# A third kind of attention step for the end: scores and one row unit together, then values, then down-projection in strips

## What is computed

```python
xn = _layernorm(x)
x = x + attn(xn) + ffn(xn)
# attn: 32 query heads and 8 key/value heads of 16; q, k, v, o are "bitnet" linears:
#   y = xn @ sign(w / s).T * (s * scale), s = max(mean(|w|), 1e-8) by row
#   scores = q k^T / 4; softmax over 1024 keys; out = softmax @ v; then the o linear
# ffn: silu(xn @ gate_w.T) * (xn @ up_w.T) @ down_w.T, inner width 1792
```

## Time and profile before

| | |
|---|---|
| median of 3 runs | 507.96 us (506.63 to 508.73) |
| the profiled execution | 507.6 us, its span 505.9 us |
| PE busy | 484.0 us, 96% of the span |
| DVE busy | 417.1 us, 82% |
| ACT busy | 352.4 us, 70% |
| POOL busy | 93.6 us, 18% |
| granted TensorE clock, mean | 0.999 |

### The profile page before, as it was taken

How to read it: one execution, slowest core, us unless ns; L and a number is a source line. 1 busy time by engine, 2 the same in 40 slices (tenths; PEclk the granted TensorE clock), 3 DMA queues, 4 the chain that set the end, 5 groups by cost and what they waited for, 6 DMA issues and landing times.

```text
span 505.9 us, 9735 instructions
## 1 busy us (share of the span) xinstructions
PE 484.0 (96%) x3882; PEld 160.9 (32%) x3882; DVE 417.1 (82%) x487; ACT 352.4 (70%) x655; POOL 93.6 (18%) x138
## 2 busy tenths in 40 slices
PE   1899999999999999999999999999999999999996
PEld 1564434434332222222222222222222223223442
DVE  7879869676779999999999999999999942223985
ACT  1943633352339999999999999999999987774000
POOL 4212244434333000000000000000000113241021
PEclk9999999999999999999999999999999999999999
DMA  8844763732005602111120220210210214452321
GB/s 275 270 86 101 164 143 43 203 67 38 6 0 75 113 26 61 41 51 36 41 61 24 43 60 23 63 40 23 62 41 24 67 36 112 110 144 78 105 72 54
DMA packets 31300, 38.99 MB, mean 77 GB/s; under 512 B 6608, under 2 KB 20816, under 8 KB 31256
## 3 DMA queue, kind: packets, MB, share of 16 engines
q1 hardware_dynamic: 22232, 27.34, 18.7%
q0 software_dynamic: 8304, 10.95, 11.6%
q10 hardware_dynamic: 720, 0.08, 0.1%
HBM read 33.24 MB, written 10.35 MB: 86 GB/s over the span
## 4 chain that ended last, share of the span: by engine, by line
PE 82%; ACT 8%; DMA 5%; DVE 2%; issue 2%; SPq 0%; ACTq 0%; DVEq 0%
PE ps L1219 24%; PE ps L1091 19%; PE ps L1184 14%; PE ps L1100 9%; PE ps L1152 8%; ACT room L674 6%; PE ps L1070 3%; PE ps L1245 3%; DMA o_scratch<-osb 2%; ACT osb L685 1%; DMA ga<-r_scratch 1%; PE ps L1008 1%; DMA hlo<-x 1%; DVE stats L733 1%; PE ps L1062 1%
## 5 line engine op out<-in xcount | busy, mean ns | idle before, releaser
L807 DVE TENSOR_REDUCE nmx<-ps 128x1 f32<-128x1024 f32 x256 | 293.7, 1217 | 14.5 <-PE ps L1100 14.3
L674 ACT ACTIVATE room<-ps 128x512 f32<-128x512 f32 x512 | 274.2, 597 | 21.2 <-PE ps L1184 11.2
L1219 PE MATMUL ps<-room,vcur 128*32 128x256 f32 (+1 forms) x1912 | 160.0, 406 | 4.4 <-ACT osb L685 4.1
L1184 PE MATMUL ps<-qst,kB 50*128 50x512 f16 x512 | 150.0, 383 | 1.0 <-DVE room L906 0.5
L1100 PE MATMUL ps<-kA,qst 48*128 48x512 f16 x512 | 145.2, 382 | 0.0
L1091 PE MATMUL ps<-room,wf 128*128 128x512 f16 x448 | 100.6, 379 | 0.0
L1219 PEld LDWEIGHTS ps<-room,vcur 128*32 128x32 f32 x1912 | 37.6, 107 | 99.7 <-issue 53.0
L1184 PEld LDWEIGHTS ps<-qst,kB 50*128 50x128 f16 x512 | 30.9, 93 | 113.0 <-ACT room L674 101.8
L655 ACT ACTIVATE room<-ps,gsc 128x512 f32<-128x512 f32 x28 | 19.2, 686 | 61.9 <-PE ps L1091 61.9
L1091 PEld LDWEIGHTS ps<-room,wf 128*128 128x128 f16 x448 | 42.4, 98 | 55.1 <-issue 7.2
L513 POOL TENSOR_TENSOR hlo<-room,hhi 128x512 f16<-128x512 f32 x28 | 34.0, 1216 | 87.7 <-ACT hhi L585 87.7
(11 more groups left out here) (127 smaller groups left out, 267.0 us busy)
## 6 DMA issues: line engine op xcount, KB each, us to landing
qst<-q_scratch SPq DMA_DIRECT2D x32, 192.0 KB, 3.6
o_scratch<-osb SPq DMA_DIRECT2D x16, 256.0 KB, 2.3
q_scratch<-parts SPq DMA_DIRECT2D x12, 256.0 KB
hlo<-x SPq DMA_DIRECT2D x8, 256.0 KB, 4.6
parts<-x POOLq DMA_DIRECT2D x8, 256.0 KB, 3.7
wf<-gate POOLq DMA_DIRECT2D x14, 128.0 KB, 4.2
wf<-up POOLq DMA_DIRECT2D x14, 128.0 KB, 5.5
wd<-down POOLq DMA_DIRECT2D x1, 1792.0 KB, 14.0
```

The source lines that it names most:

```text
L674: nc.scalar.activation(probs[:, s % 2, r, :], ps[:, score_bank(entry(j, i)), :], ACT.Exp, scale=gam_reg[par][r]).then_inc(scores_free, 1)
L807: nc.vector.tensor_reduce(nmx[:, hf, idx:idx + 1], bank_pair(idx % 2), AX.X, ALU.max, negate=True).then_inc(rows_free, 1)
L1184: nc.tensor.matmul(ps[:, score_bank(e), :], kB[low:low + SROWS, par, kt % (TT // 2) * P:(kt % (TT // 2) + 1) * P], qst[low:low + SROWS, pa ...
L1219: mm = nc.tensor.matmul(ps[32 * r:32 * r + 32, 7, of], vcur[:, par, key_tile(r, j), :], probs[:, s % 2, r, of], start=(j == 0 and part == ...
```

## The change

From step 107 on (`LATE`) a third kind of step, `late_scores`, takes the place of the others. It issues four scores (banks 4, 5, 6 and 3), then, up to step 116, one row unit (always banks 0 and 1), then all values, then as many down matmuls as `QUOTAS` says: 3 in each of steps 107 to 114, 2 in 115 and 116, 7 in 117 to 124, then 10, 9 and 9. Each of these down matmuls becomes four (`down_strips`) with 32 output columns each, which write 32 partitions of the bank each. Tiles 0 and 2 go to bank 2, tiles 1 and 3 to bank 1.

The 10 row units that steps 107 to 111 held two at a time are now in steps 107 to 116 one at a time, so the last block's maxima are transposed in step 116 (`LATE_T_STEP`) and not in 113. With that, POOL issues unit 1 ahead of the split of the last maximum, and SP stores block 13 before it waits for the last shift. VectorE takes finished down tiles at 21, 25, 29 and ahead of that step's row unit. The output projection's first four tiles use the banks in the order 0, 3, 2, 1, and wait for what used them last.

```diff
-    D_OUT = [20, 24, 28]
+    D_OUT = [21, 25, 29]
+    LATE_SCORES = [4, 5, 6, 3]
+    LATE_T = 0
+    LATE_T_STEP = 4
+    FILL_BANKS = [2, 1]
+    O_BANK = [0, 3, 2, 1]
+    LATE = (NG - 1) * STEPS - 5
+    ROWS_END = LATE + (2 * NG * UNITS - 2 * UNITS - 2 * LATE)
+    QUOTAS = [3] * 8 + [2] * 2 + [7] * 8 + [10, 9, 9]
...
@@ sync: half_ended
-                if not last or par == 0:
+                if not last or (par == 0 and hf == 0):
                     load_shift(v + 2, 1 - par, hf)
                 sp.wait_ge(pv_free, v + 3)
                 sp.dma_start(o_scratch[bass.ds(g * (REP * 2 * D), REP * 2 * D), hf * HALF:(hf + 1) * HALF],
                              osb[:, hf, :]).then_inc(osb_free[hf], 16)
+                if last and par == 0 and hf == 1:
+                    load_shift(v + 2, 1 - par, hf)
@@ gpsimd
-            normalize_io(pool, 0)
+            for u in range(2):
+                normalize_io(pool, u)
             split_max(2 * NG - 1, 1)
-            for u in range(1, QT - 1):
+            for u in range(2, QT - 1):
                 normalize_io(pool, u)
@@ vector: step_rows
+                if step < LATE:
                     row_max(ga_ * (2 * UNITS) + hf * UNITS + 2 * j, hf, 2 * j)
                     row_max(ga_ * (2 * UNITS) + hf * UNITS + 2 * j + 1, hf, 2 * j + 1)
+                elif step < ROWS_END:
+                    unit = 2 * UNITS + LATE + step
+                    dve.wait_ge(rows_ready, unit + 1)
+                    nc.vector.tensor_reduce(nmx[:, 1, unit % UNITS:unit % UNITS + 1], bank_pair(0), AX.X, ALU.max,
+                                            negate=True).then_inc(rows_free, 1)
@@ tensor
+            def down_strips(i, f, part):
+
+                if f == 0 and part == 0:
+                    if i == 0:
+                        pe.wait_ge(wd_loaded, 16)
+                        pe.wait_ge(rows_free, 2 + 2 * UNITS + 2 * LATE)
+                    elif i == 1:
+                        pe.wait_ge(rows_free, 2 + NG * 2 * UNITS)
+                    else:
+                        pe.wait_ge(ff_ready, i - 1)
+                for c in range(P // 32):
+                    lo = i * P + c * 32
+                    mm = nc.tensor.matmul(ps[32 * c:32 * c + 32, FILL_BANKS[i % 2], :], (hhi, hlo)[part][:, f, lo:lo + 32],
+                                          wd[:, f, :], start=(f == 0 and part == 0),
+                                          stop=(f == FT - 1 and part == 1))
+                    if f == FT - 1 and part == 1:
+                        mm.then_inc(down_strips_ready, 1)
...
+            def late_scores(gp, s):
+
+                gp_, par, hf, j = at(gp, s)
+                step = gp * (2 * STEPS) + s
...
+                for i, r in enumerate(ROUND):
+                    kt = key_tile(r, j)
+                    low = kt // (TT // 2) * HI
+                    if step > LATE:
+                        pe.wait_ge(scores_free, 3 + (step - 1) * REP + i + 1)
+                    elif LATE_SCORES[i] == 3:
+                        pe.wait_ge(rows_free, 2 + 2 * UNITS + 2 * LATE)
+                    else:
+                        pe.wait_ge(scores_free, 3 + last_use[LATE_SCORES[i]])
+                    nc.tensor.matmul(ps[:, LATE_SCORES[i], :],
+                                     kB[low:low + SROWS, par, kt % (TT // 2) * P:(kt % (TT // 2) + 1) * P],
+                                     qst[low:low + SROWS, par, hf, r, :], start=True, stop=True).then_inc(scores_ready, 1)
+                if step < ROWS_END:
+                    unit = 2 * UNITS + LATE + step
+                    pe.wait_ge(rows_free, 2 + unit)
+                    for b in range(2):
+                        mm = nc.tensor.matmul(ps[:, b, :],
+                                              qst[b * HI:b * HI + KROWS, 1, 1, unit % UNITS // (HALF // P),
+                                                  unit % (HALF // P) * P:(unit % (HALF // P) + 1) * P],
+                                              kA[b * HI:b * HI + KROWS, 1, :], start=True, stop=True)
+                    mm.then_inc(rows_ready, 1)
+                times_values(gp, s - 1, 0, 1)
+                for fill in fills_of(step):
+                    down_strips(*fill)
+                if step == ROWS_END - 1:
+                    transpose_max(2 * NG - 1, 1, LATE_T)
```

More of the change, by code:

```diff
@@ L121, in layer_kernel, with t_step, fills_of, bank_of @@
     assert (BLOCK + 1) % 3 == 0
+    LATE_SCORES = [4, 5, 6, 3]
[6 more added lines that the diff above has]
+    QUOTAS = [3] * 8 + [2] * 2 + [7] * 8 + [10, 9, 9]
+    assert LATE % TT > T_STEP and ROWS_END - 1 == (2 * NG - 2) * TT + LATE_T_STEP
+    assert LATE + len(QUOTAS) == NG * STEPS and sum(QUOTAS) == len(FILLS) and sum(QUOTAS[:ROWS_END - LATE]) == 2 * FT
+    def t_step(block_):
+        return LATE_T_STEP if block_ == 2 * NG - 2 else T_STEP
+    def fills_of(step):
+        done = sum(QUOTAS[:step - LATE])
+        return FILLS[done:done + QUOTAS[step - LATE]]
+    def bank_of(gp, s, i):
+        if gp * 2 * STEPS + s >= LATE:
+            return LATE_SCORES[i]
+        return score_bank(entry(s % TT, i))
     def exps_before(e):
@@ L668, in exps @@
                 step = gp * (2 * STEPS) + s
-                if j == T_STEP + 1 and not (last and s >= STEPS + TT):
-                    take_max(gp * 4 + s // TT + 1, score_bank(T_ENTRY))
+                if j == t_step(step // TT) + 1 and not (last and s >= STEPS + TT):
+                    take_max(gp * 4 + s // TT + 1, LATE_T if step >= LATE else score_bank(T_ENTRY))
                 act.wait_ge(probs_free, step + 1)
@@ L1155, in down_proj, with scores @@
                     mm.then_inc(down_ready, 1)
-            def scores(gp, s, last, opening=False):
+            def scores(gp, s, opening=False):
                 gp_, par, hf, j = at(gp, s)
@@ L1165, in scores @@
                         pe.wait_ge(kB_loaded[par], 32 * (gp_ + 1))
[L1166 to L1173 removed]
+                    if block_ < 2 * NG - 2:
+                        pe.wait_ge(q_loaded[1 - par][hf], 32 * (gp_ + par + 1))
+                        if hf == 0:
+                            pe.wait_ge(kA_loaded[1 - par], 32 * (gp_ + par + 1))
                 for i, r in enumerate(ROUND):
@@ L1195, in scores @@
                             half_rows(1 - par, hf, idx, half).then_inc(rows_ready, 1)
-                    if i % 2 == 1 and with_rows and not opening:
+                    if i % 2 == 1 and not opening:
                         times_values(gp, s - 1, i // 2, 2)
-                    elif i == 1 and not with_rows:
-                        times_values(gp, s - 1, 0, 1)
-                    elif i == REP - 1 and not with_rows:
-                        for n in fill:
-                            down_proj(*FILLS[n])
@@ L1226, in _ @@
             pe.wait_ge(kones_ready, 2)
-            scores(0, 0, False, opening=True)
-            for gp in range(NP - 1):
-                for s in range(2 * STEPS):
-                    scores(gp, s + 1, False)
-            for s in range(2 * STEPS - 1):
-                scores(NP - 1, s + 1, True)
+            last_use = {}
+            for step in range(LATE):
+                for i in range(REP):
+                    last_use[bank_of(step // (2 * STEPS), step % (2 * STEPS), i)] = step * REP + i + 1
+            scores(0, 0, opening=True)
+            for step in range(1, LATE):
+                scores((step - 1) // (2 * STEPS), (step - 1) % (2 * STEPS) + 1)
+            for step in range(LATE, NG * STEPS):
+                late_scores((step - 1) // (2 * STEPS), (step - 1) % (2 * STEPS) + 1)
             times_values(NP - 1, 2 * STEPS - 1, 0, 1)
```

53 lines of the change are left out of this document (28 added, 25 removed).

## The result

The changed kernel took 508.97 us (median of 20 executions, 507.44 to 511.09) where the kernel before took 507.27 (506.58 to 511.41): a ratio of 1.0026, with a 95% interval of 1.0015 to 1.0037. (The two medians are 1.7 us apart; the ratio, formed from all the runs, makes it 1.3, and I go by the ratio.) The change is 1.3 us slower, within the 0.5% that I called no change, and on the other side of zero from my forecast of 1.0 us faster. The profiled execution took 508.86 us, its span 507.1, at a mean clock of 0.996. One later execution of the changed kernel, of 911.5 us, is far outside all others and is left out of every ratio.

What follows compares the result with a forecast made beforehand. TensorE and the DMA round trip into the last exponentials bound the kernel. Shorter steps less 3.5 us of waits put the last values 1.1 us earlier, taken as -1.0 on 507.96: 507.0 us; own case 505.5 to 509.5, 8 in 10 503.5 to 511.5.

Steps and rivals of the forecast that it cites:

- A late step: Steps 117 to 127: with seven sets of strips 3.02 us against 3.26; steps 107 to 114, with three sets, 2.38.
- A set of strips: Four 32-column loads and four matmuls side by side: 0.216 us, loads hidden; own range up to 0.235.
- strips that don't hide their loads: Rival: a set costs 0.32 us, adding 9 us in steps 117 to 127; about 517 us; chance 0.17.
- no saving per step: Rival: going from fp32 values to fp16 strips costs 0.14 us, a late step takes 3.16; 508.1 us; chance 0.10.
- The entry: Start of the new steps, delayed a little by banks: step 107 at 398.85 us, 108 at 401.3, 115 at 418.2.
- VectorE's order: Row units queue behind unit 0's normalization, which awaits a 7.5 us broadcast load; TensorE waits in step 116, costing 3.5 us.
- the rival in which VectorE doesn't hold: Normalization of unit 0 finds its data, step 117 begins at 422.8; gain 4.6 us, 503.4 us; chance 0.17.
- The finished tiles: Down tiles VectorE takes at steps 117, 121 and 125: complete by then, VectorE idle there, so they cost nothing.
- the one on the last maximum: Last block's shift: rows land some 2.5 us after SP's issues, at 432.5; step 120 wants them at 435.4: 3 us cover.
- the last of my three signs of being wrong: Sign that the forecast fails: the last block's shift lands after step 119.
- The fourth rival: Block 13's store, unit 1's loads and shifts meet; each broadcast load takes 1 to 2 us more; 509 to 511; chance 0.08.
- The sum: End of the steps: last values begin at 461.25 us, right behind the last exponentials, before at 462.4; -1.1 us.

Runs made afterwards that it cites:

- the product behind the row units: Changed kernel, but VectorE normalizes unit 0 after step 116's row unit and takes its low half at step 117; ratio to before 1.0066, 511.36 us.
- lists alone: Changed kernel with VectorE's and ScalarE's normalization work moved to earlier places, POOL's order as in the change; ratio to before 0.9992, 507.38 us.
- control: The changed kernel itself, unchanged, run again beside the experiments; ratio to before 1.0047 (510.24 us), a further time 1.0036 (509.67 us).
- the last version: Changed kernel, normalization moved earlier, unit 1's product after 22, unit 2's loads issued before unit 1's broadcast load, unit 0's halves after 18; ratio 0.9947, 504.98 us.
- the first version with unit 1 later: Changed kernel, normalization earlier, unit 2's loads before the last maximum's split, unit 1's product after 22, halves after 23; ratios 0.9969 (506.12 us), again 0.9951 (505.22 us).

## Why the prediction was wrong

**What held.** A late step: 3.045 for 3.02, and 2.40 for 2.38. A set of strips: 0.216, loads hidden, no price for going from values to strips. So two of my rivals fell, strips that don't hide their loads and no saving per step; whole down matmuls in the new order, and strips in the old, say how much each half of the saving is. The entry: step 107 at 2.91 for 2.93, step 108 at 5.50 for 5.38, step 115 at 22.34 for 22.28. VectorE's order: its broadcast load issued at 17.60 (forecast 17.58) took 7.07 us (7.5), TensorE waited in step 116, and step 117 began at 30.53 for 30.43; the product behind the row units measured those waits at 3.6 us for 3.5. So the rival in which VectorE doesn't hold fell too. The finished tiles cost nothing. That step 117 came within 0.10 us is in part luck: the load was 0.43 us quicker than I took it, VectorE ended the last row unit at 29.78 and not at 30.18, and the half clock, which I had not priced, took those 0.40 us back.

**The step that failed** is the one on the last maximum: "the rows take some 2.5 to land", "that is 3 us of cover". The forecast had SP's issues right (the last ended at 34.4 against 34.1), but the last of the four took another 6.7 us to be complete: it landed at 41.08 and not at 36.6. Step 120 began at 41.17, where 39.83 would have followed on step 119. That the shift lands after step 119 was the last of my three signs of being wrong. The 2.5 was the median landing over eight issues, and step 120 waits for the last of four, not for the median: in the trace of before the first three of that shift landed in 2.5 to 2.7 us, the last did not. (The profile counts from the start of an issue; I added the 2.5 behind its end, which erred by 0.6 us the other way.) With 10 us of cover there it cost nothing. The same view of the kernel before, the last write of the last shift alone:

```profile
qst<-shp SPq DMA_DIRECT2D x1, 4.0 KB, 5.7
```

It landed at 29.24, 5.1 us after SP was done, beside unit 1's numerator load issued at 22.38. That row was there to be looked for. I moved the shift by 10 us to a place where unit 2's numerator load stands beside it in just the same way, and priced it by the median. The run that held the load back shows the cause: 3.5 us for 7.3. With the numerator load beside it but the broadcast load landed it was 4.9 (lists alone) and 5.7 (before); 7.3 came with both in flight. The fourth rival, "the DMA chain slips", had the shifts meeting the loads in it, but placed the loss on the broadcast loads, which kept their 7 us.

**A second term was missing**: the clock. TensorE idles 1.84 us in step 116 and then runs 3.41 us at half clock. I had the wait and no price for what follows it; it is some 0.6 us here, as most of it hides behind VectorE.

**The sum.** The forecast was 65.33 for the last values and 66.92 was measured, 1.59 later. Step 117 is 0.10 later; step 117 itself takes 0.18 more, of which 0.16 is the clock; 0.03 more in each of steps 118 and 119; 1.34 is the wait at step 120; and from step 120 on it goes 0.10 faster than forecast (25.75 for 25.85). Against before, -1.1 becomes +0.5.

**What stays open.** The ratio says +1.3 us [0.8, 1.9] in the first measurement and 1.8 and 2.4 in the others. From step 105 to the last values the three traces of the changed kernel are 0.5 to 0.75 us behind the first trace of the kernel before and 1.0 to 1.2 behind the second; what follows the last values takes 43.5 us in all five. In the first pair of traces another 0.8 us lie ahead of step 105 (396.73 against 395.92), in code that both share. These starts run from 395.92 to 397.33 in the five traces and up to 401.21 in the experiments, in part by stretches of half clock at about 155 us. Whether the change bears on them, by the number of its instructions or otherwise, wasn't tried.

The half clock in step 116 is not what makes the change slower by itself. Of the changed kernel's 43 executions seven had a mean granted clock of 0.999 or 1.000; 3.41 us at half clock would bring it to 0.997. These seven took 508.3 us on average, and the 32 such executions of the kernel before, beside the two controls, took 507.3. The time of the kernel with the lists alone also is better than its trace says.

## What to carry to other kernels

A small DMA that something waits for is priced by what else is in flight when it goes out, read from the same DMA in the trace of before, each issue by itself and not as a median; and one with ample cover should be looked at before its cover is taken away. An engine that works in order hands on its wait: three times here (the product ahead of row units, POOL's wait ahead of unit 2, ScalarE's high half) a wait that was removed came back in the next thing queued. When two waits lie one behind the other, find the later one first: removing the 3.6 us in step 116 gained nothing, while moving the loads away from the shift and the lists with them made it 0.5% faster than before.

## What the runs showed of the hardware

The landing of the last of four writes of 4 KB, from the start of its issue: 2.4 us in the last version, where the 512 KB numerator load had landed, 3.5 with that load held back, 4.9 in the kernel with the lists alone, 5.7 in the kernel before and 7.3 in the changed one with that load issued among them. In all 15 traces in which such a load was in flight at the last write, that write was complete between 0.5 us before the load and 1.1 us after it: at 29.24 and 28.76 in the kernel before, 41.08 and 41.38 in the changed one, 36.60 and 35.90 in the first version with unit 1 later.

The Trainium skill, "TensorE: Matmul & The Clock Gate", "Part 3", ties overlapping weight loads to differing row groups or to a background weight buffer; here the loads of strips, which all use 128 rows, stayed hidden: a set of four took 0.216 us, as one matmul of full width does, in all of the 112 sets but the two that ran at half clock.

TensorE's clock was at 0.50 for 3.41 us behind waits of 1.84 us (1.97 in the control) in step 116 and of 2.27, and for 6.83 us behind one of 4.93. It stayed at 1.00 behind 1.61 and 0.74 in the same step, behind 1.68 in the last version, and behind 2.00 ahead of step 120 with whole down matmuls. So a wait on TensorE's path of about this length can cost up to 1.7 us more than itself, where the matmuls behind it aren't hidden (step 117 took 4.73 us instead of 3.05 with the row unit behind the strips), and it need not; what decides isn't shown here.
